# Moving two output tiles and half a projection stage inside the block loop of a linear-attention and soft-MoE kernel

## The reference, cut to what matters

```python
q = mlp(x, W1q, b1q, W2q, b2q)          # mlp(x) = gelu(x @ W1 + b1) @ W2 + b2
k = mlp(x, W1k, ...)                    # every width is 1024, T = 8192
v = mlp(x, W1v, ...)
scores = (q @ k.T) / sqrt(1024 * 2048) * tril(ones(T, T))     # no softmax
attn = layernorm(scores @ v) * ln_w + ln_b
x = layernorm(x + attn)

xn = layernorm(x) * ln_gamma + ln_beta                        # soft mixture of experts
logits = l2norm(xn) * scale @ l2norm(mu)                      # 16 experts x 16 slots = 256 columns
slot_in = softmax(logits over the tokens).T @ xn
slot_out = expert_mlp(slot_in)
x = layernorm(x + softmax(logits over the slots) @ slot_out)
```

## Time and profile before

| | us |
|---|---|
| median of the runs shown (2 runs: 5647.22 and 5700.03) | 5673.62 |
| the profiled execution | 5640.99 |
| its span, slowest core | 5639.4 |
| its span, fastest core | 5628.9 |
| PE matmul busy | 3001.6 (53%) |
| ACT busy | 1685.7 (30%) |
| DVE busy | 1307.2 (23%) |

### The profile page before, as it was taken

One profiled execution on the slowest core, in us unless ns is written; L12 is line 12 of the kernel. 1 busy time (PEld: TensorE's weight loads), 2 busy tenths in 40 slices (PEclk: granted clock), 3 DMA queues, 4 the chain that ended last, 5 costly groups with the idle time before them and its releaser, 6 DMA issues.

```text
span 5639.4 us, 38733 instructions; the slowest of 8 cores (5628.9 to 5639.4 us)
## 1 busy us (share of the span) xinstructions
PE 3001.6 (53%) x11729; PEld 1204.5 (21%) x11945; DVE 1307.2 (23%) x1862; ACT 1685.7 (30%) x3056; POOL 173.5 (3%) x299
## 2 busy tenths in 40 slices
PE   0006766666666666665667576666666662522121
PEld 0002322222222222222223222222222221100000
DVE  0000231313222222131222223131312233033333
ACT  0002323242424242424233333323242423122222
POOL 1000000000000000000000000000000000000000
PEclk9999877787878777777878787877787775555555
DMA  9995221212111121212121212121211101322222
GB/s 112 115 119 129 63 65 50 65 50 65 65 50 66 48 81 48 69 45 83 48 66 52 75 52 65 50 65 50 65 63 51 65 13 34 113 73 79 76 75 74
DMA packets 228013, 379.60 MB, mean 67 GB/s; under 512 B 78786, under 2 KB 96210, under 8 KB 226402
## 3 DMA queue, kind: packets, MB, share of 16 engines
q1 hardware_dynamic: 210738, 287.39, 15.9%
q0 software_dynamic: 17072, 89.71, 9.8%
HBM read 352.46 MB, written 101.19 MB: 80 GB/s over the span
## 4 chain that ended last, share of the span: by engine, by line
PE 41%; DVE 21%; ACT 16%; issue 10%; another core or an unknown queue 5%; SPq 3%; DMA 3%; DVEq 1%; ACTq 1%; POOL 1%; POOLq 0%
PE pSA L450 8%; PE pSB L450 7%; DVE st L71 4%; ACT st L71 4%; PE pAT L556 3%; ACT jb L71 3%; DMA exp_in<-expb 3%; DVE slot_in L71 3%; DVE tB L71 3%; DVE tA L71 3%; PE pOa L669 2%; SPq L391 2%; PE pSA L455 2%; PE pSB L603 2%
## 5 line engine op out<-in xcount | busy, mean ns | idle before, releaser
L450 PE MATMUL pSA<-x_fm,wbufA 128*128 128x512 bf16 x1507 | 412.6, 421 | 394.3 <-ACT hbuf L71 218.7
L450 PE MATMUL pSA<-hbuf,wbufB 128*128 128x512 bf16 x1023 | 295.8, 441 | 183.2 <-ACT q_fm L71 113.5
L450 PE MATMUL pSB<-x_fm,wbufA 128*128 128x512 bf16 x1502 | 382.9, 396 | 1.8
L1247 PE MATMUL pTR<-identS,exp_in 128*128 128x128 bf16 x128 | 23.8, 289 | 532.2 <-DMA exp_in<-expb 532.2
L450 PEld LDWEIGHTS pSA<-x_fm,wbufA 128*128 128x128 bf16 x1536 | 157.0, 104 | 614.7 <-issue 466.6
L71 DVE TENSOR_TENSOR st<-st 128x2 f32<-128x2 f32 x192 | 30.8, 160 | 1094.3 <-ACT st L71 378.5
L556 PE MATMUL pAT<-q_fm,k_fm 128*128 128x512 bf16 x496 | 186.7, 543 | 143.5 <-DVE xn_bf L71 93.1
L450 PE MATMUL pSB<-hbuf,wbufB 128*128 128x512 bf16 x992 | 258.5, 403 | 1.7
L71 ACT ACTIVATE jb<-xn_bf 128x1024 bf16<-128x1024 bf16 x64 | 67.6, 1056 | 527.5 <-DVE at_s L71 439.1
L71 DVE TENSOR_TENSOR tA<-tB,lnw_b 128x2048 f32<-128x2048 f32 x32 | 73.4, 2292 | 600.1 <-ACT tB L71 600.1
L603 PE MATMUL pSA<-v_tm,k_tm 128*128 128x512 bf16 x496 | 150.9, 424 | 103.3 <-DVE S L71 102.8
(11 more groups left out here) (161 smaller groups left out, 4525.2 us busy)
## 6 DMA issues: line engine op xcount, KB each, us to landing
wbufA<-wb SPq DMA_DIRECT2D x48, 2048.0 KB, 9.7
wbufB<-wb SPq DMA_DIRECT2D x48, 2048.0 KB, 9.6
OUT<-out_sb SPq DMA_DIRECT2D x64, 512.0 KB, 3.4
xb<-x POOLq DMA_DIRECT2D x1, 16384.0 KB, 156.6
x_tm<-xb SPq DMA_DIRECT2D x16, 1024.0 KB, 5.7
xprime<-xp_t POOLq DMA_DIRECT2D x64, 256.0 KB, 2.3
xp_in<-xprime POOLq DMA_DIRECT2D x64, 256.0 KB, 2.8
w1eb<-w1e POOLq DMA_DIRECT2D x1, 8192.0 KB, 85.6
```

The costliest lines, as they stand in the source:

```text
L450: mm = t.matmul(p[:, :], wbuf[:, kc, m * 128:(m + 1) * 128], src[:, kc, :], start=(kc == 0), stop=(kc == NCH - 1))
L1247: mm = t.transpose(pTR[:, ec * 128:(ec + 1) * 128], exp_in[:, par, ec * 128:(ec + 1) * 128], ident[:, :])
```

## The change

Four edits to phase A:

1. O(0) and O(1) of block b + 1 are no longer written at the head of the next loop body, but between AT and supd of block b + 1, at the end of the body for b. They wait for scast, by a new wait in `emit_O`. Only block 0 keeps its two at the head.
2. Stage 3.1 moves up from behind ffn(0), ffn(1) to just behind chain segment 12 of c01. Every later stage part of the body moves up by one place against the c23 chain; kT goes ahead of c23's segment 11 and AT ahead of segment 12.
3. scast is written in three pieces (3, 3 and 2 copies), ahead of O(0), instead of two of 4.
4. ffn(2) and ffn(3) use pTR and pAT as ffn(0) and ffn(1) do, since pOa and pOb now hold O(0) and O(1) of the next block; their waits follow.

```diff
 (emit_O)
                 W(t, "t", V, v_at_evac if exact_ow else None)
                 W(t, "t", V, v_ffn_end.get(b * NT - 1))
+                W(t, "t", V, v_after_scast.get(b - 1))
 (emit_ffn)
-            if ti < 2:
-                pX = pTR[:, :].bitcast(F32)
-                pDen = pTR[:, 512:516].bitcast(F32)
-                pATb = pAT[:, :].bitcast(BF16)
-            else:
-                half = slice((ti - 2) * 512, (ti - 1) * 512)
-                pX = pOa[:, half]
-                pDen = pOa[:, (ti - 2) * 512 + 256: (ti - 2) * 512 + 258]
-                pATb = pOb[:, half].bitcast(BF16)
+            pX = pTR[:, :].bitcast(F32)
+            pDen = pTR[:, 512:516].bitcast(F32)
+            pATb = pAT[:, :].bitcast(BF16)
...
-                elif ti == 1:
+                elif ti == 2:
+                    if (b + 1) in v_atev:
+                        W(t, "t", V, v_atev[b + 1])
+                    else:
+                        W(t, "t", V, v_xnfm[tile64 - 1])
+                else:
                     W(t, "t", V, v_xnfm[tile64 - 1])
...
-                if ti == 1:
+                if ti in (1, 2, 3):
                     W(t, "t", V, v_ffn_end.get(tile64 - 1))
 (the loop body)
-        emit_O(0, v_at_evac=v_atev[b])
-        emit_O(1, v_at_evac=v_atev[b])
+        if b == 0:
+            emit_O(0, v_at_evac=v_atev[b])
+            emit_O(1, v_at_evac=v_atev[b])
...
             EMIT("N", lambda: emit_stage(b + 1, 3, 0))
-            crun(c01, 12, 14)
+            crun(c01, 12, 13)
+            EMIT("N", lambda: emit_stage(b + 1, 3, 1))
+            crun(c01, 13, 14)
             EMIT("L", lambda: emit_ffn(0))
             EMIT("L", lambda: emit_ffn(1))
             crun(c23, 0, 3)
-            EMIT("N", lambda: emit_stage(b + 1, 3, 1))
+            EMIT("G", lambda: emit_stage(b + 1, 4, 0))
             crun(c23, 3, 5)
-            EMIT("G", lambda: emit_stage(b + 1, 4, 0))
+            EMIT("G", lambda: emit_stage(b + 1, 4, 1))
             crun(c23, 5, 7)
-            EMIT("G", lambda: emit_stage(b + 1, 4, 1))
+            EMIT("N", lambda: emit_stage(b + 1, 5, 0))
             crun(c23, 7, 9)
-            EMIT("N", lambda: emit_stage(b + 1, 5, 0))
+            EMIT("N", lambda: emit_stage(b + 1, 5, 1))
             crun(c23, 9, 11)
-            EMIT("N", lambda: emit_stage(b + 1, 5, 1))
+            emit_kT(b + 1)
             crun(c23, 11, 12)
-            emit_kT(b + 1)
+            emit_AT(b + 1)
             crun(c23, 12, 13)
-            emit_AT(b + 1)
+            scast_seg(b, 0, 3)
+            scast_seg(b, 3, 6)
+            scast_seg(b, 6, NCH)
+            emit_O(0, b=b + 1, v_at_evac=v_atev[b + 1])
             crun(c23, 13, 14)
-            scast_seg(b, 0, 4)
-            scast_seg(b, 4, NCH)
+            emit_O(1, b=b + 1, v_at_evac=v_atev[b + 1])
             for s in supd_segs(b + 1):
                 s()
             emit_xtm(b + 1)
```

## The result

| | before | changed |
|---|---|---|
| median of all runs, us | 5670.63 (10 runs) | 5490.35 (11 runs) |
| lowest run, us | 5638.45 | 5487.65 |
| ratio, with its 95% interval | | 0.9711 [0.9671, 0.975] |
| body length on core 5, us | 268.4 | 258.3 |
| table loads | 93 | 123 |

What follows compares the result with a forecast made beforehand. No engine is full; PE streams or idles behind the ACT/DVE epilogue chain. Per body 15.5 - 16.2 + 10.3 = 9.6 us, 134 over 14 bodies, -0.7 and 15.8 outside: 149 us, forecast 5498 us, range 5440 to 5560.

Steps and rivals of the forecast that it cites:

- Stage 3.1 into the wait: Stage 3.1 fills PE's 9.8 us wait ahead of ffn(0); ffn(0) starts 1.6 us late, gain by stage 4.0 is 7.2 us.
- The stages against c23, two new loads: Stages 4 and 5, one place up: one load costs the chain 1.3 us, the other is hidden; gain so far 6.7 us.
- The rival in which the chain eats 4.7 us a body: Stages 4 and 5: second load on the chain, slow start and hand-overs lose 4.7 us a body; 5568 us, chance 0.09.
- kT and AT: End of stage 5: kT ahead of c23's segment 11, AT ahead of segment 12, lengths kept; gain so far 15.5 us.
- AT warms early: Rival at kT and AT: upper clock in two slow AT groups, with kT up to 5 us a body; 5423 us, chance 0.08.
- Behind AT: From AT's last emptying to ffn(2): 11.6 us wait, 12.3 for O(0) and O(1), 16.3 for supd; loss 16.2 us.
- low clock behind AT: Rival behind the new wait: O(0) and O(1) would show a clock near 0.5 to their end; chance 0.09.
- slower run: Case that the changed kernel is slower than before; chance 0.04.
- The head: Head of the body: stage 0 follows two O tiles instead of four, 12.3 for 22.6 us; gain 10.3 us.
- Outside the fourteen bodies: Body 0 keeps O(0), O(1) at its head, -0.7 us; block 15's chain follows ffn(3) at once, gain 15.8 us.

Runs made afterwards that it cites:

- e10: The changed kernel with two more table loads a body ahead of c23's segment 3, each followed by a one-column operation: ratio to before 0.9755, lowest run 5511.06 us.
- e11: Control of e10: the changed kernel with two one-column operations at that place and no load: ratio to before 0.9755, lowest run 5480.07 us.
- e5: The changed kernel with all three pieces of scast ahead of c23's segment 12 instead of behind it: ratio to before 0.9714.
- e8: e5 with emit_O waiting for the end of ffn(3) only where that is already written down: ratio to before 0.957, a body 5.2 us shorter than e5's.
- e3: The kernel before with only O(0) and O(1) moved, with the new ffn banks and the wait for scast: ratio to before 1.0038.
- e4: The changed kernel with O(0) and O(1) back at the head, the old banks and scast in two pieces: ratio to before 0.9712, lowest run 5458.03 us.
- e7: e4 with scast moved early, into DVE's idle time ahead of c01's segment 12: ratio to before 0.9474, lowest run 5365.53 us.
- e9: The changed kernel with scast ahead of c01's segment 12 and emit_O waiting for ffn(3) only where already written down: ratio to before 0.9342, lowest run 5278.11 us.

## Why the prediction was right, point by point

The steps of the forecast, measured on core 5 as means over 14 bodies, in us. "Predicted" is the gain by the forecast's own replay.

| step of a body | before | changed | gain | predicted |
|---|---|---|---|---|
| stage 0 to ffn(0) | 83.6 | 86.3 | -2.7 | -1.6 |
| ffn(0) to the last v_tm emptying | 82.1 | 73.6 | 8.5 | 8.3 |
| from there to kT | 4.4 | 0.7 | 3.7 | 4.1 |
| kT to AT's last emptying | 28.8 | 22.3 | 6.6 | 4.7 |
| from there to ffn(2) | 23.6 | 40.0 | -16.4 | -16.2 |
| ffn(2) to stage 0 | 45.9 | 35.4 | 10.6 | 10.3 |
| body | 268.4 | 258.2 | 10.2 | 9.6 |

(The rows are rounded one by one; by the x_tm loads the gain is 10.1.)

- **Stage 3.1 into the wait.** Right. The wait ahead of ffn(0) is 4.54 us (about 4.5 was named). The step costs 2.7 us up to ffn(0) and not 1.6. The traces of core 5 account for the missing 1.1 us. Some 0.4 come from the body that was replayed: its wait was 9.80 us, that of most bodies 9.45. The rest is the clock ahead of this step, which the forecast took as unchanged: of thirteen bodies before, five reached ffn(0) in 82.4 us, with fewer slow groups in stages 1 and 2 than the others had (about 84.3); in the changed kernel all take 86.0 to 86.7.
- **The stages against c23, two new loads.** Right. The waits are 4.88 and 5.88 us where the replay had 4.9 and 6.0, and e10 against e11 bears out that a load costs at most 1.3 us (two of them 1.9 us a body). The rival in which the chain eats 4.7 us a body did not come: this step gained 8.5 us.
- **kT and AT.** Right in mechanism, the term mis-sized: 6.6 us gained for 4.7. The forecast kept kT's four rounds at 8.0 us and AT at 15.0. In most blocks kT behind stage 5 starts with PE at its upper level, 0.61 us for 8 transposes and not 1.01, and a round then takes 1.62 us and not 2.02, so that AT starts 7.3 us behind kT and not 8.1. AT, from its first matmul to the end of its last emptying, takes 15.1 us instead of 15.9 (means of fifteen blocks). That is a part of the rival "AT warms early", 1.9 us of its 5.
- **Behind AT.** Right in size. The wait is 12.17 us (11 to 12 named; counted from AT's last emptying, as the forecast did, it is 11.3 us for 11.6), O(0) and O(1) start slow and take 13.0 us for the 12.3 of the forecast (1624.12 to 1637.15), and supd runs in 16.3 us (1637.15 to 1653.48), as worked out. But the cause was only half told. The forecast wrote that "O(0) waits for all that stands on DVE behind AT", and laid it to segment 12 standing ahead of the copies. e5 shows a second wait that covers the same work, and e8 that without it the order of the two does matter. Since both end together in the changed kernel, no term of the sum could show it.
- **The clock behind the long wait.** The chances give 0.09 to a low clock behind AT and 0.04 to a slower run; neither came. The windows over O(0) and O(1) and over supd show a granted clock of 0.78 and then 1.00:

```profile
1624.10:1636.40 12.30, 12.28 (x45) 5.08 (x46) 0.00 (x0) 3.09 (x7) 0.00 (x0) 0.78 0.70 171
1636.40:1652.50 16.10, 14.70 (x65) 5.21 (x62) 9.68 (x14) 0.00 (x0) 0.00 (x0) 1.00 0.01 2
```

- **The head.** Right, 10.6 for 10.3.
- **Outside the fourteen bodies.** Mis-sized. The forecast had -0.7 us ahead of them and 15.8 behind; core 5 shows 3.4 and 10.9. The bodies give 141.6 where it had 134. The first load's place differs by several us from core to core of one run (807.56 on core 0, 811.69 on core 5), so the 3.4 is not firm. The sum is 156 us on this core in the profiled runs and 151 between the lowest runs, for 149. That the total is this close is in part luck: 7.6 us too little in the bodies and 4.9 too much behind them go against each other. The time, 5498, lies some 10 us above the lowest run because it was counted from 5647 us and not from the lowest.

The forecast weighed the change as a whole, and did not say which edit carries it. Its own terms told. Of the 16.2 us lost behind AT, 4.8 are segment 12, which the second edit puts there with or without the tiles; the other 11.4 stand against 10.3 gained at the head, so the moved tiles lose about 1 us a body, and all else is a gain. e3 (1.2 us) and e4 (2.3 us) confirm this.

## What to carry to other kernels

When a step is moved, its waits move with it, and each has to be read again at the new place: what stands queued ahead of the instruction that it waits for, and whether the bookkeeping that it looks up has been written yet. A lookup that can come back empty must not mean "wait for everything"; in a trace such a wait shows as a releaser whose result the instruction does not read, and it hides for as long as another wait ends later. Moving PE work behind a wait in order to cover other work pays only if that PE work does not wait for it too: the copies had first to go where DVE was idle (6.8 us a body in e7), and then the same two tiles that had cost 2.3 us a body were worth 4.4.

## What the runs showed of the hardware that was not expected

- A wait of PE does not always bring the lower clock. In the changed kernel the third group of stage 3.0 comes back behind 2.51 us at the upper level, stage 4.1 behind 4.88 us at the lower (row at 1816.30):

```profile
1760.22 1.89 PE L450 MATMUL pSA<-hbuf,wbufB 128*128 128x512 bf16 x8 [2.51 <-ACT k_fm L71]
```

- But the length of the wait does not settle it. On core 5 the upper level holds behind this wait of stage 3.0 in all fifteen blocks. In stage 1.0, at the same place and behind the same wait (2.5 us, in two blocks 2.8, at both places), it holds in seven; in the other eight the groups turn slow within the first two:

```profile
1929.97 2.48 PE L450 MATMUL pSA<-hbuf,wbufB 128*128 128x512 bf16 x8 [2.51 <-ACT q_fm L71]
1932.25 3.02 PE L450 MATMUL pSB<-hbuf,wbufB 128*128 128x512 bf16 x8
```

- The level also falls where PE hardly waits. In the body shown kT's first three rounds take 0.61 us for 8 transposes and the last 1.01 (rows at 1850.98 and 1855.84), with 1.01 us of idleness between rounds, and AT's first group behind them is slow (3.57 us, row at 1857.86). The same 1.01 us between AT's groups of 8 full matmuls leaves the level up once it is reached (groups of 1.89 us): in e9 on core 5 PE goes on at it from there through O(0) (4 matmuls in 1.02 us, 8 in 1.89), O(1) and supd, where no matmul takes over 0.38 us. How many of AT's groups are slow differs from block to block, and it goes with the place in kT where the level fell. In nine blocks of e9 on core 5 the third round of kT is still faster than 1.01 us (0.61 to 0.84), and each of these blocks has one slow group in AT; the six whose third round takes 1.01 us have three. In the changed kernel the five blocks with a fast third round have one, and eight of the other ten have three. What makes the level fall earlier was not tried.
